# Low halves of the second output weights made on GpSimd, and the last tile stored in two halves

## What is computed

```
x = x + tanh(g_xattn) * (attention(layernorm(x), ctx) @ Wo + bo)      # 8 heads of 64, softmax over 77
x = x + tanh(g_ffn) * ffn(layernorm(x))
ffn(y) = q(relu(q(q(y) @ q(w1).T + q(b1)))) @ q(w2).T + q(b2)          # 256 -> 1024 -> 256
q(v) = clip(round(v * scale), -128, 127) / scale                       # 8-bit fixed point
```

## Time and profile before

| | |
|---|---|
| median of 3 runs | 118.89 us (118.67 to 119.33) |
| the profiled execution | 118.80 us |
| its span | 117.0 us |
| PE, PEld, DVE busy | 112.3, 103.2, 96.2 us |
| ACT, POOL busy | 77.9, 87.9 us |
| granted TensorE clock, mean | 1.0 |

### The profile page before, as it was taken

The page is one execution under the profiler, slowest core; times in us unless marked ns, Lnnn a source line. Parts: engine busy times, 40 slices in busy tenths (PEclk is TensorE's granted clock), DMA queues, the critical chain, the costliest instruction groups (busy, mean ns, idle before and its releaser), DMA issues.

```text
span 117.0 us, 2916 instructions
## 1 busy us (share of the span) xinstructions
PE 112.3 (96%) x1021; PEld 103.2 (88%) x1021; DVE 96.2 (82%) x222; ACT 77.9 (67%) x173; POOL 87.9 (75%) x161
## 2 busy tenths in 40 slices
PE   7699999999999999999999999999999999999990
PEld 2399979999899999989999999999999999897880
DVE  3049889999999788999999999999797979648982
ACT  3138579887979889994848484848483828548420
POOL 5003739878785899898989989995999999989720
DMA  3998699400000000000020002000200020020105
GB/s 86 328 379 286 249 377 382 170 8 0 3 0 6 0 3 0 0 6 0 0 90 0 6 0 90 0 6 3 90 0 8 0 90 0 0 88 7 61 32 179
DMA packets 5712, 8.87 MB, mean 76 GB/s; under 512 B 1191, under 2 KB 2242, under 8 KB 5698
## 3 DMA queue, kind: packets, MB, share of 16 engines
q1 hardware_dynamic: 5466, 8.34, 20.2%
q10 hardware_dynamic: 232, 0.34, 0.8%
HBM read 6.59 MB, written 2.10 MB: 74 GB/s over the span
## 4 chain that ended last, share of the span: by engine, by line
PE 61%; POOL 26%; DMA 3%; issue 3%; DVE 3%; ACT 1%; SPq 0%; POOLq 0%; DVEq 0%; ACTq 0%
PE sc_ps L935 16%; PE of_ps L985 15%; PE h_ps L1016 7%; POOL probs L313 6%; POOL hid L375 5%; POOL x_sb L404 5%; PE of_ps L1031 4%; PE tr_ps L949 4%; DMA wk_sb<-in_L_xattn_Wk_dram 3%; POOL yq L329 3%; POOL rstd L323 3%; PE tr_ps L1031 1%; POOL rstd L309 1%; PE sc_ps L1031 1%; POOL u_sb L350 1%
## 5 line engine op out<-in xcount | busy, mean ns | idle before, releaser
L935 PE MATMUL sc_ps<-a_sb,xT 128*128 128x308 f32 x192 | 31.3, 312 | 0.0
L985 PE MATMUL of_ps<-u_sb,pT 128*128 128x256 f32 x240 | 31.2, 281 | 0.0
L985 PEld LDWEIGHTS of_ps<-u_sb,pT 128*128 128x128 f32 x240 | 29.6, 188 | 0.2
L935 PEld LDWEIGHTS sc_ps<-a_sb,xT 128*128 128x128 f32 x192 | 27.5, 188 | 0.7 <-ACT xT L449 0.4
L517 ACT ACTIVATE hid_q<-h_ps,b1z 128x256 int8<-128x256 f32 x58 | 24.5, 487 | 3.6 <-PE h_ps L1016 3.6
L466 ACT ACTIVATE probs<-probs,rstd 128x616 f32<-128x616 f32 x16 | 13.1, 817 | 19.1 <-DVE probs L670 18.8
L313 POOL TENSOR_TENSOR probs<-probs,rden 128x616 f32<-128x616 f32 x16 | 19.5, 1221 | 4.4 <-DVE rden L685 4.4
L375 POOL CAST hid<-hid_q 128x512 bf16<-128x512 int8 x27 | 15.8, 611 | 2.0 <-ACT hid_q L517 2.0
L1016 PE MATMUL h_ps<-x2T,w1T 128*128 128x256 bf16 x128 | 16.7, 274 | 0.0
L662 DVE TENSOR_REDUCE mx<-sc_ps 128x8 f32<-128x616 f32 (+1 forms) x18 | 13.0, 720 | 2.6 <-PE sc_ps L935 2.2
L670 DVE TENSOR_TENSOR probs<-sc_ps,mx 128x616 f32<-128x616 f32 (+1 forms) x18 | 13.1, 728 | 1.4
(11 more groups left out here) (141 smaller groups left out, 177.6 us busy)
## 6 DMA issues: line engine op xcount, KB each, us to landing
w_sb<-in_L_ffn_w_dram SPq DMA_DIRECT2D x2, 1024.0 KB, 11.2
out_dram<-x_sb SPq DMA_DIRECT2D x7, 256.0 KB, 2.0
x_sb<-in_x_dram SPq DMA_DIRECT2D x4, 256.0 KB, 6.4
x_sb<-in_x_dram SPq DMA_DIRECT2D x1, 1024.0 KB, 11.4
wq_sb<-in_L_xattn_Wq_dram SPq DMA_DIRECT2D x1, 512.0 KB, 5.2
wv_sb<-in_L_xattn_Wv_dram SPq DMA_DIRECT2D x1, 512.0 KB, 6.3
wo_sb<-in_L_xattn_Wo_dram SPq DMA_DIRECT2D x1, 512.0 KB, 6.9
wk_sb<-in_L_xattn_Wk_dram SPq DMA_DIRECT2D x1, 256.0 KB, 3.9
```

The source lines that it names most:

```text
L935: ins = nc.tensor.matmul(sc_ps[:, a, 0:HALF], xT[:, T % 2, p, c, :], a_sb[:, q, T // TB, c, HALF * a:HALF * a + HALF], start=first, stop=last)
L985: ins = nc.tensor.matmul(attn_ps, pT[:, T % 2, p, P * c:P * c + P], u_sb[:, q, MC * (T // TB) + c, :], start=first, stop=last)
```

## The change

Four things are changed in the steps 1 to 4, and one at the end.

- The low parts of batch 1's `u_sb`, pieces 0 and 1, are no longer made by TensorE and ScalarE. ScalarE copies each whole bank to `u_whole` in step 2, between its high parts, and POOL subtracts, piece 0 in step 2 and piece 1 in step 3. Piece 2 stays as it was.
- The low part of tile 4's probabilities is made by VectorE, no longer by TensorE and ScalarE (`LOW_FROM_PSUM`).
- The second half of w2 is rounded by ScalarE in step 3, no longer by POOL.
- POOL's `output_bias` stands in step 1, no longer in step 2.
- The result of tile 15 leaves in two transfers, partitions 0 to 63 from SyncE and 64 to 127 from ScalarE, behind its last activation.

With them go the semaphores: VectorE's centring counts one for each instruction (`centred` gives the counts), and the waits on the low parts name POOL's.

```diff
-LOW_FROM_PSUM = (3, 4)
-POOL_HALVES = (1,)
+LOW_FROM_PSUM = (3,)
...
+        def centred(T, bank):
+
+            return 2 * T + bank + 1 if T < 2 else T + 3
...
-            for T in range(TILES - 2, TILES):
-                sp.wait_ge(result_ready, T + 1)
-                sp.dma_start(out_v[:, T // TB, T % TB // 2, T % 2, :], x_sb[:, T, :]).then_inc(stored, 16)
-            sp.wait_ge(stored, 16 * (TP + 1))
+            sp.wait_ge(result_ready, TILES - 1)
+            sp.dma_start(out_v[:, 1, TB // 2 - 1, 0, :], x_sb[:, TILES - 2, :]).then_inc(stored, 16)
+            sp.wait_ge(result_ready, TILES)
+            sp.dma_start(out_v[0:P // 2, 1, TB // 2 - 1, 1, :], x_sb[0:P // 2, TILES - 1, :]).then_inc(stored, 16)
+            sp.wait_ge(stored, 16 * (TP + 2))
...
             def u_low(b, n):
                 pool.wait_ge(u_high, 3 * b + n + 1)
-                pool.wait_ge(u_copied, 1)
+                pool.wait_ge(u_copied, 1 if b == 0 else 2 + n)
...
-                if s == 2:
+                if s == 1:
                     output_bias()
-                if s == 3:
-                    round_w2(1)
+                if s in (2, 3):
+                    u_low(1, s - 2)
...
             def u_copy_whole(b, n):
                 act.wait_ge(u_psum, 3 * b + n + 1)
+                if (b, n) == (1, 1):
+                    act.wait_ge(u_low_pool, 1)
                 nc.scalar.copy(u_whole[:, n, :], u_banks[b, n]).then_inc(u_copied, 1)
...
-                if s >= 4 and s in LOW_FROM_PSUM:
-                    pT_low_copy(s)
...
                 if s == 2:
-                    for n in range(3):
+                    for n in range(2):
                         u_copy(1, n)
+                        u_copy_whole(1, n)
+                    u_copy(1, 2)
                     round_weights(w2_in, w2_sb, w2q, w2_rounded, (0,))
                 if s == 3:
-                    for n in range(2):
-                        u_low_copy(n)
+                    u_low_copy()
                     pT_low_copy(3)
-                    u_low_copy(2)
+                    round_weights(w2_in, w2_sb, w2q, w2_rounded, (1,))
...
             hidden_round(K_LAST + 3, 0)
+            act.wait_ge(result_ready, TILES)
+            act.dma_start(out_v[P // 2:P, 1, TB // 2 - 1, 1, :], x_sb[P // 2:P, TILES - 1, :]).then_inc(stored, 16)
...
             def output_weights_rest():
                 pe.wait_ge(consts, 4)
-                for n in range(3):
-                    pe.wait_ge(u_high, 4 + n)
-                    subtract_high(u_banks[1, n], u_of(1, n, 0), u_rest)
+                pe.wait_ge(u_high, 6)
+                subtract_high(u_banks[1, 2], u_of(1, 2, 0), u_rest)
...
                 if k == 0:
                     pe.wait_ge(w1T_ready, 2)
-                    pe.wait_ge(u_low_act, 2)
+                    pe.wait_ge(u_high, 5)
+                    pe.wait_ge(u_copied, 3)
```

More of the change, by code:

```diff
@@ L366, in bias_rows @@
                 else:
-                    pool.wait_ge(u_low_act, 1)
+                    pool.wait_ge(u_low_pool, 2)
                 nc.gpsimd.tensor_copy(u_sb[0:1, :, MC * b, :], bo_parts[:, :, :].bitcast(F32)).then_inc(bo_rows, 1)
@@ L382, in hidden_bias @@
                 nc.gpsimd.tensor_scalar(b1z[:, :], b1q[:, :], AQ / WQ, 1.0, ALU.mult, ALU.mult).then_inc(b1_ready, 1)
[L384 to L390, removed]
             def output_bias():
@@ L464, in exponentials @@
                 act.wait_ge(rstd1_ready, T + 1)
-                act.wait_ge(centered, 2 * T + 2)
+                act.wait_ge(centered, centred(T, 1))
                 nc.scalar.activation(probs_v(T), probs_v(T), ACT.Exp, scale=rstd1[:, T:T + 1]).then_inc(exp_done, 1)
@@ L489, in u_copy, with u_low_copy @@
                 nc.scalar.copy(u_of(b, n, 0), u_banks[b, n]).then_inc(u_high, 1)
-            def u_low_copy(n):
-                act.wait_ge(u_rest, n + 1)
-                nc.scalar.copy(u_of(1, n, 1), u_banks[1, n]).then_inc(u_low_act, 1)
+            def u_low_copy():
+                act.wait_ge(u_rest, 1)
+                nc.scalar.copy(u_of(1, 2, 1), u_banks[1, 2]).then_inc(u_low_act, 1)
             def pT_copy(T):
@@ L672, in subtract_maxima @@
                                         mx[:, i, h].rearrange("p (a h) -> p a h", a=len(banks)).unsqueeze(3)
-                                        .to_broadcast([P, len(banks), H // 2, M]), ALU.subtract).then_inc(centered, len(banks))
+                                        .to_broadcast([P, len(banks), H // 2, M]), ALU.subtract).then_inc(centered, 1)
             def center(T, banks=(0, 1)):
@@ L861, in output_window @@
                 start, stop = not two or j % 2 == 0, not two or j % 2 == 1
-                if b == 1:
-                    start = start and col == 0
                 return nc.tensor.matmul(u_banks[b, bank][row:row + WIN, col:col + D], vz[rows, b, j, at:at + WIN],
-                                        wo_sb[rows, j, :], start=start, stop=stop, skip_group_check=b == 1,
+                                        wo_sb[rows, j, :], start=start, stop=stop,
                                         tile_position=(HD * q, row))
@@ L926, in scores @@
                     if T >= 1:
-                        pe.wait_ge(centered, 2 * T - 1 + a)
+                        pe.wait_ge(centered, centred(T - 1, a))
                     for p, q in PARTS:
@@ L973, in attend @@
                 if T == TB:
-                    pe.wait_ge(u_low_act, 3)
+                    pe.wait_ge(u_low_act, 1)
+                    pe.wait_ge(u_low_pool, 3)
                     pe.wait_ge(bo_rows, 2)
@@ L994, in quantisedT @@
                 else:
-                    pe.wait_ge(centered, 2 * TILES)
+                    pe.wait_ge(centered, centred(TILES - 1, 1))
                     if T - 2 in yT_last:
```

## The result

The changed kernel took 120.37 us (median of 4 runs, 119.61 to 121.5) against 118.78 us for the kernel before beside it: a ratio of 1.0106, 95% interval 1.0068 to 1.0145. It is 1.1 to 1.3 us slower. The forecast was 119.2 with 0.60 for no change; the time lies outside its range of 118.5 to 119.7. Its mechanism in the middle of the program is there, at 0.34 and 0.47 us in two executions where 0.45 was forecast; the term that the forecast put at zero, the store, is larger (0.53).

The account below looks back on a forecast made before the run. PE is dense, but POOL's run to hidden(1) was taken to decide at PE's ffn_out(0). 118.80 + 0.2 (exp(4) late) + 0.25 (POOL's subtraction) + 0 (PE, VectorE, store) = 119.25, given as 119.2; range 118.5 to 119.7 us.

Parts of the forecast that it names:

- Its mechanism in the middle of the program: Up to PE's ffn_out(0): exp(4) 0.2 us late plus POOL's subtraction 0.25 us longer, together +0.45 us.
- What bounds the middle: Around 34 to 52 us: POOL's hidden(1) holds PE at ffn_out(0), so PE's removed 0.83 us counts 0.
- ScalarE's two copies: Tile step 2: two added copies push ScalarE back 0.96 us against 0.60 idle; exp(4) and POOL's start 0.2 us later.
- POOL's subtraction for the rounding: POOL, step 3: a 1.29 us subtraction replaces the 1.04 us rounding of w2's second half, +0.25 us, bounds 0 and 0.5.
- VectorE's extra low part: VectorE, step 4: tile 4's added low part of 0.78 us fits idle waits of 0.88 us; cost 0, up to 0.78.
- ScalarE's step 3: Two low copies go and w2's second rounding (1.11 us) comes; only exp(5) is about 0.2 us later, cost 0.
- The output bias: POOL, moved from step 2 to step 1: tile 3's softmax 0.39 us later, which PE does not see.
- The semaphore counts: VectorE's centring: the new counts move no instruction.
- The store: Program end, tile 15's two halves: taken as 0, between 0.2 us won and 0.25 us lost.
- ScalarE's slow first issue: Last store, a rival with chance 0.14: ScalarE's issue takes 0.62 instead of 0.37 us, end 0.25 later, 119.5 us.
- The prediction's own sign of being wrong: Program end: the forecast is wrong if last result to end moves by more than 0.2 us.
- The possible gain that the Trainium skill names: Last store: with idle DMA engines smaller pieces may finish sooner, -0.2 us if it holds.

Follow-up runs that it names:

- the run with more on POOL: The kernel before plus one unneeded 128x616 copy on POOL in step 3, behind its rounding of w2; ratio 1.0024 (0.9985 to 1.0063).
- The run with w2 later: The changed kernel with the old store and ScalarE's w2 roundings moved to step 3 and the end of step 4; ratio 0.9982 to the kernel before.
- the two halves from SyncE: The kernel before with tile 15 stored as two halves of 64 partitions, both issued by SyncE one after the other; ratio 1.0074 (1.0042 to 1.0105).

## Why the prediction was wrong

- *What bounds the middle: right.* PE's removed 0.83 us gained nothing in the changed kernel. POOL's hidden(1) holds PE in ffn_out(0), as the 0.17 us of the earlier trace rows said; the run with more on POOL shows it directly.
- *ScalarE's two copies: right.* 0.48 us each, exp(4) 0.2 us late against exp(3) (5.34 us behind it, before 5.14), idle time gone. The run with w2 later takes the term away.
- *POOL's subtraction for the rounding: right in direction, too large.* 1.31 for 1.04 us, but 0.15 more up to tile 5's softmax instead of 0.25. POOL's lines show where the rest went: the rounding began 0.78 us after the start of the 1/sqrt in front of it (39.98 to 40.76), the subtraction 0.67 (40.54 to 41.21); from there to the softmax it is 1.01 and 1.27. The forecast compared the two lengths alone.
- *VectorE's extra low part, ScalarE's step 3: right, no cost seen.* The forecast's 0.45 for the middle measured 0.34 and 0.47 in two executions.
- *The output bias: no cost at the end, but not unseen by PE.* Tile 3's softmax is 0.62 us later behind exp(3) (2.59, before 1.97), not 0.39, and PE waits 0.35 us for the `yq` behind it. This took what pieces 0 and 1 spared PE.
- *The semaphore counts: wrong, by a little and to the good.* "The new counts of the semaphore for centring move no instruction" left out 0.05 us for each centring from tile 2 on, 0.10 up to exp(3).
- *The store: the step that failed.* "In the rows the 128 KB already occupy all of the engines while they move, so I take 0", with a loss of 0.25 at most, from ScalarE's slow first issue. It measured 0.51 to 0.53 us, outside both bounds, by 64 partitions and not by the queue: 0.2 us in the issue, the rest up to the landing. What the forecast took as fixed, that halves keep the issue and the latency of the whole and move at its rate, did not hold: the issue grew from at most 0.37 to 0.54 us, and a half occupies the engines for 0.55 x 0.50 = 0.28 us also where it moves alone (each of the two halves from SyncE, 116.5 to 117.0 and 117.2 to 117.7), where half of the 0.40 was to be expected. The prediction's own sign of being wrong, a move of over 0.2 us from the last result to the end, is there. No row before showed a transfer of 64 partitions, and the nearest (a small load of 77 partitions at the start, 0.62 us from ScalarE) was read as a cold queue; the same load for the other batch was issued by SyncE in 0.41 us, so that row shows neither. With 0.5 in its place the sum is 118.80 + 0.45 + 0.5 = 119.75, slower by more than 0.5%, which the range missed as well. By the first ratio 118.80 becomes 120.06, with an interval of 119.61 to 120.52, which holds that sum.
- *The two rules on splitting.* The rule of the Trainium skill, DMA: Bandwidth & Descriptors, Rules for kernel authors, not to split by partition halves, held. The possible gain that the Trainium skill names in Perfetto Trace Analysis, DMA Optimizations, did not come, by partitions (+0.51 us) or by columns (+0.11, little more than an unsplit store varies by).

## What to carry to other kernels

An engine that is dense on the chain gains nothing from less work where another engine's result meets it a few steps on with little to spare: look for the small wait (here 0.17 us) and follow its engine back to its last real wait; what is added to that run is paid nearly one to one. Put one-time pieces where that engine idles, and check what it would wait for next before counting the whole of what is taken off it. Price a transfer by one of the same shape; for a shape that the trace does not hold, leave the bound open upward.

## What the runs showed that was not expected

- A store of 64 partitions x 1 KB was issued in 0.54 to 0.59 us, one of 128 partitions x 1 KB in 0.33 to 0.37, 128 x 512 B in 0.37. Two halves of 64 took 0.54 us of all 16 engines, the whole 0.40.
- ScalarE's transfer queue, unused for 114 us, issued in 0.35 us.
- A VectorE subtraction that counts its semaphore up by one began 0.05 us sooner behind the maximum in front of it than the same one that counts it up by two (five profiles of the one, seven of the other).
- The start of the program varied by over a microsecond between executions of the same order, while later distances repeated within 0.06 us to hidden(1) and 0.14 to the last result; those told apart terms of 0.2 us that the timed runs could not.
